# Three tiles of the third product in parts on even steps, and the left product rounded ahead of the relu of layer 0

## The reference

```python
e = stack([tbl_f[ids[:, f]] for f in range(32)], axis=1)        # (1024, 32, 64)
x0 = h = e
for i in (0, 1):
    z = einsum('bhd,bmd->bhmd', h, x0).reshape(batch, H * M, dim)
    out = relu(einsum('bcd,oc->bod', z, Ws[i]) + bs[i])          # 128 outputs
    # layer 0: the first 64 outputs are h of layer 1, the last 64 are a result
    # layer 1: all 128 are results
z = sum(concat(results, axis=1), axis=-1)                        # (1024, 192)
h = concat([z, dense_ctx], axis=1)
y = relu(relu(h @ W_top1 + b_top1) @ W_top2 + b_top2) @ W_top3
```

## Time and profile before

| | |
|---|---|
| median of 3 runs | 2003.78 us (2003.62 to 2006.34) |
| time of the profiled execution | 2002.59 us |
| its span on the core | 2000.7 us |
| mean granted TensorE clock | 0.997 of full speed |
| busy: TensorE, VectorE, ScalarE, GpSimd | 98%, 96%, 84%, 87% |
| mean traffic of DMA | 182 GB/s |

### The profile page before, as it was taken

How to read it: one execution, slowest core, us unless ns; L and a number is a source line. 1 busy time by engine, 2 the same in 40 slices (tenths; PEclk the granted TensorE clock), 3 DMA queues, 4 the chain that set the end, 5 groups by cost and what they waited for, 6 DMA issues and landing times.

```text
span 2000.7 us, 28399 instructions
## 1 busy us (share of the span) xinstructions
PE 1954.1 (98%) x7112; PEld 1338.9 (67%) x7112; DVE 1915.6 (96%) x1230; ACT 1687.7 (84%) x1943; POOL 1731.0 (87%) x708
## 2 busy tenths in 40 slices
PE   2999999999999999999999999999999999999998
PEld 0667666666666666666666666666676676676664
DVE  3999999999999999999999999999999999999991
ACT  2888888888888888888888888888888888888883
POOL 3998998998998998998998989989989989989871
PEclk9999999999999999999999999999999999999999
DMA  7998788788788788788887887887887887887820
GB/s 190 220 213 192 182 191 194 179 194 192 179 194 191 183 192 189 184 192 187 187 194 183 189 192 183 191 193 180 193 193 178 195 191 180 194 193 180 191 62 0
DMA packets 268305, 364.13 MB, mean 182 GB/s; under 512 B 107506, under 2 KB 107890, under 8 KB 268163
## 3 DMA queue, kind: packets, MB, share of 16 engines
q1 hardware_dynamic: 258338, 352.61, 77.5%
q0 software_dynamic: 8192, 8.40, 1.6%
q10 hardware_dynamic: 1760, 2.96, 0.5%
HBM read 347.02 MB, written 16.78 MB: 182 GB/s over the span
## 4 chain that ended last, share of the span: by engine, by line
PE 91%; POOL 4%; issue 2%; SPq 1%; DMA 1%; ACT 0%; DVE 0%; POOLq 0%
PE out L629 58%; PE out L613 20%; PE out L620 10%; POOL zl L217 4%; PE out L615 1%; SPq L259 0%; PE out L677 0%; DMA fields_dram<-emb 0%; POOL emb L200 0%; PE hrep L677 0%; SPq L284 0%; SPq L269 0%; PE out L670 0%; PE z L670 0%; PE hrep L670 0%
## 5 line engine op out<-in xcount | busy, mean ns | idle before, releaser
L217 POOL TENSOR_TENSOR zl<-prod,zh 128x2048 fp32r<-128x2048 f32 (+1 forms) x384 | 1473.2, 3866 | 144.2 <-ACT zh L372 144.1
L629 PE MATMUL out<-zh,w1h 128*128 128x512 f32 x1792 | 752.7, 420 | 5.5 <-DVE zl L512 4.4
L629 PE MATMUL out<-zl,w1h 128*128 128x512 f32 x1792 | 700.1, 391 | 0.0
L629 PE MATMUL out<-zh,w1l 128*128 128x512 f32 x1792 | 698.8, 390 | 0.0
L372 ACT ACTIVATE zh<-prod 128x2048 fp32r<-128x2048 f32 (+1 forms) x384 | 623.0, 1623 | 40.4 <-DVE prod L557 23.2
L385 ACT ACTIVATE hrep<-out,b_sb 32x512 f32<-32x512 f32 (+1 forms) x768 | 496.2, 646 | 131.9 <-PE out L615 122.1
L613 PE MATMUL out<-prod,w_sb 128*128 128x512 f32 x1024 | 464.6, 597 | 35.2 <-DVE prod L495 30.2
L629 PEld LDWEIGHTS out<-zh,w1h 128*128 128x128 f32 x1792 | 337.2, 188 | 130.4 <-issue 60.3
L629 PEld LDWEIGHTS out<-zh,w1l 128*128 128x128 f32 x1792 | 337.1, 188 | 97.8 <-issue 30.4
L629 PEld LDWEIGHTS out<-zl,w1h 128*128 128x128 f32 x1792 | 336.6, 188 | 73.8
L613 PEld LDWEIGHTS out<-prod,w_sb 128*128 128x128 f32 x1024 | 195.2, 191 | 232.3 <-issue 222.5
(11 more groups left out here) (61 smaller groups left out, 736.7 us busy)
## 6 DMA issues: line engine op xcount, KB each, us to landing
rot_low<-fields_dram SPq DMA_DIRECT2D x512, 256.0 KB, 6.7
rot_high<-fields_dram SPq DMA_DIRECT2D x512, 256.0 KB, 4.4
xrep<-fields_dram SPq DMA_DIRECT2D x256, 128.0 KB, 3.9
fields_dram<-emb SPq DMA_DIRECT2D x512, 32.0 KB, 5.3
left_x<-fields_dram SPq DMA_DIRECT2D x256, 64.0 KB, 2.9
left_y<-fields_dram SPq DMA_DIRECT2D x256, 64.0 KB, 2.2
emb<-in_tables,idx POOLq DMA_INDIRECT x256, 5.0
w_sb<-in_w ACTq DMA_DIRECT2D x1, 1024.0 KB, 6.2
```

The source lines that it names most:

```text
L217: pool.tensor_tensor(zl[u][:, :, :], product[:, 0:SIZES[u], :], zh[u][:, :, :].bitcast(F32), ALU.subtract).then_inc(zl_made[u], 1)
L629: mm = nc.tensor.matmul(out1[:, :], w[:, k, :], z[:, t, :], start=start and t == 0 and part == 0, stop=stop and t == SIZES[u] - 1 and part ...
```

## The change

Unit 2 gets three tiles of `prod[3]` in even steps and keeps two in odd ones; the whole tiles are then one in even steps and two in odd ones. ScalarE's rounding and GpSimd's subtraction of the unit are made as long as that. `round_left` moves on ScalarE from the start of the odd step, behind the copy of x, to the end of the even step before it, between `replicate_h1` and the relu of layer 0 (L402). The order on the other engines stays.

```diff
-SPLITS = (tiles(P1, 0, 4), tiles(P2, 0, 4), tiles(P3, 0, 2), tiles(P4, 0, 2), tiles(P4, 2, 4))
-SIZES = (4, 4, 2, 2, 2)
-FIRST = (0, 4, 8, 10, 12)
+SPLITS = (tiles(P1, 0, 4), tiles(P2, 0, 4), tiles(P3, 0, 3), tiles(P4, 0, 2), tiles(P4, 2, 4))
+SIZES = (4, 4, 3, 2, 2)
+FIRST = (0, 4, 8, 11, 13)
-WHOLE3 = tiles(P3, 2, 4)
+def in_parts(u, b):
+    return SIZES[u] - (u == 2 and b == 1)
...
-            def low_part(m, u, product):
+            def low_part(m, u, size, product):
...
-                pool.tensor_tensor(zl[u][:, :, :], product[:, 0:SIZES[u], :], zh[u][:, :, :].bitcast(F32),
+                pool.tensor_tensor(zl[u][:, 0:size, :], product[:, 0:size, :], zh[u][:, 0:size, :].bitcast(F32),
                                    ALU.subtract).then_inc(zl_made[u], 1)
...
-                act.activation(zh[u][:, :, :], product, ACT.Copy).then_inc(zh_made[u], 1)
+                act.activation(zh[u][:, 0:size, :], product[:, 0:size, :], ACT.Copy).then_inc(zh_made[u], 1)
...
-                if b == 1 and is_up_to(i, c, LAST - 1):
-                    round_left(i * 2 + (c + 1) // 2)
...
                 if is_up_to(i, c, LAST - 1):
                     replicate_h1(m + 1)
+                if b == 0 and is_up_to(i, c, LAST - 2):
+                    round_left(i * 2 + (c + 2) // 2)
+                if is_up_to(i, c, LAST - 1):
                     finish_l0(m + 1, 1 - b, i * 2 + (c + 1) // 2)
...
-            def whole(tiles, product, used):
-                for t in range(2):
-                    mm = nc.tensor.matmul(out1[:, :], w1_sb[:, tiles.start + t, :], product[:, t, :],
+            def whole3(m, b):
+                pe.wait_ge(p3_made, m + 1)
+                for t in range(in_parts(2, b), LOW):
+                    mm = nc.tensor.matmul(out1[:, :], w1_sb[:, tiles(P3, t, t + 1).start, :], prod[3][:, t, :],
                                           start=False, stop=False)
...
-            def split(m, u, start=False, stop=False):
+            def split(m, b, u, start=False, stop=False):
+                size = in_parts(u, b)
                 pe.wait_ge(zl_made[u], m + 1)
-                for t in range(SIZES[u]):
+                for t in range(size):
```

More of the change, by code:

```diff
@@ L227, in step @@
                     number_rows(n, b)
-                low_part(m, 0, prod[1])
-                low_part(m, 1, prod[2])
-                low_part(m, 2, prod[3])
+                low_part(m, 0, in_parts(0, c % HALVES), prod[1])
+                low_part(m, 1, in_parts(1, c % HALVES), prod[2])
+                low_part(m, 2, in_parts(2, c % HALVES), prod[3])
             pool.wait_ge(ids_loaded, 32)
@@ L366, in round_left, with round_split @@
                 act.activation(left_parts[:, :], lz[:, :], ACT.Copy).then_inc(left_rounded, 1)
-            def round_split(m, u, made, product):
+            def round_split(m, u, size, made, product):
                 act.wait_ge(made, m + 1)
@@ L411, in step @@
                     copy_left(i * 2 + (c + 2) // 2)
-                if b == 1 and is_up_to(i, c, LAST - 1):
-                    round_left(i * 2 + (c + 1) // 2)
-                round_split(m, 0, p1_made, prod[1][:, :, :])
-                round_split(m, 3, z4_made[0], z4[:, :, :])
+                round_split(m, 0, in_parts(0, b), p1_made, prod[1])
+                round_split(m, 3, in_parts(3, b), z4_made[0], z4)
                 if is_past(i, c, 0):
                     finish_l1(m - 1, 1 - b, i * 2 + (c + 1) // 2 - 1)
-                round_split(m, 1, p2_made, prod[2][:, :, :])
+                round_split(m, 1, in_parts(1, b), p2_made, prod[2])
                 if is_up_to(i, c, LAST - 1):
                     replicate_h0(m + 1)
-                round_split(m, 2, p3_made, prod[3][:, 0:SIZES[2], :])
-                round_split(m, 4, z4_made[1], z4[:, :, :])
+                round_split(m, 2, in_parts(2, b), p3_made, prod[3])
+                round_split(m, 4, in_parts(4, b), z4_made[1], z4)
                 if is_up_to(i, c, LAST - 1):
                     replicate_h1(m + 1)
+                if b == 0 and is_up_to(i, c, LAST - 2):
+                    round_left(i * 2 + (c + 2) // 2)
+                if is_up_to(i, c, LAST - 1):
                     finish_l0(m + 1, 1 - b, i * 2 + (c + 1) // 2)
@@ L616, in matmuls_l0 @@
                                  start=False, stop=True).then_inc(l0_done, 1)
-            def whole(tiles, product, used):
-                for t in range(2):
-                    mm = nc.tensor.matmul(out1[:, :], w1_sb[:, tiles.start + t, :], product[:, t, :],
+            def whole3(m, b):
+                pe.wait_ge(p3_made, m + 1)
+                for t in range(in_parts(2, b), LOW):
+                    mm = nc.tensor.matmul(out1[:, :], w1_sb[:, tiles(P3, t, t + 1).start, :], prod[3][:, t, :],
                                           start=False, stop=False)
-                mm.then_inc(used, 1)
-            def split(m, u, start=False, stop=False):
+                mm.then_inc(whole3_used, 1)
+            def split(m, b, u, start=False, stop=False):
+                size = in_parts(u, b)
                 pe.wait_ge(zl_made[u], m + 1)
-                for t in range(SIZES[u]):
+                for t in range(size):
                     k = FIRST[u] + t
@@ L629, in split @@
                         mm = nc.tensor.matmul(out1[:, :], w[:, k, :], z[:, t, :], start=start and t == 0 and part == 0,
-                                              stop=stop and t == SIZES[u] - 1 and part == 2)
+                                              stop=stop and t == size - 1 and part == 2)
                 mm.then_inc(split_used[u], 1)
@@ L635, in step @@
                 if is_past(i, c, 0):
-                    split(m - 1, 1)
-                    split(m - 1, 4)
-                    split(m - 1, 2, stop=True)
+                    split(m - 1, 1 - c % HALVES, 1)
+                    split(m - 1, 1 - c % HALVES, 4)
+                    split(m - 1, 1 - c % HALVES, 2, stop=True)
                 if is_up_to(i, c, LAST - 1):
@@ L642, in step @@
                     pe.wait_ge(relu1_made, m)
[L643 to L646, removed]
+                split(m, c % HALVES, 3, start=True)
+                split(m, c % HALVES, 0)
+                whole3(m, c % HALVES)
             pe.wait_ge(w0_folded, 4)
@@ L658, in _ @@
                 step(ITERS - 1, c)
-            split(LAST, 1)
-            split(LAST, 4)
-            split(LAST, 2, stop=True)
+            split(LAST, 1, 1)
+            split(LAST, 1, 4)
+            split(LAST, 1, 2, stop=True)
             pe.wait_ge(top_loaded, 96)
```

## The result

The changed kernel takes 1999.47 us in the median, the kernel before 2003.55 us, 20 runs each. The ratio is 0.9982 with a 95% interval of 0.9976 to 0.9988: 3.6 us less, between 2.4 and 4.8 (the medians themselves differ by 4.1). The profiled execution took 2000.27 us, with a span of 1998.4.

A forecast was written before the change was run, and what follows sets the result against it. TensorE was taken to bound the kernel at 29.92 us a pair, with VectorE's 29.875 taking over: 64 x (29.92 - 29.875) = 2.9 us less, so 2000.9 us predicted, range 1998.8 to 2003.9.

The forecast's parts named there:

- What bounds the kernel before: Over a pair of steps, TensorE sets the pace at 29.92 us; VectorE alone needs 29.875.
- TensorE's saving: In even steps, one whole tile becomes three float32r matmuls, saving 0.174 us; TensorE's pair falls to 29.75.
- VectorE's floor of 29.875: VectorE's own pair, read soon after the start where it catches up; it becomes the longest pair after the change.
- the gaps: Three late starts on VectorE around L505, 0.37 us a pair; moving the rounding gains 0.00. Rival that they close: chance 0.10.
- GpSimd: Subtracting three tiles takes 3.49 us, 1.11 more in even steps; its work becomes 29.07 a pair, under 29.875.
- ScalarE: Rounding three tiles takes 1.48 us, 0.45 more; `round_left` doesn't wait, and unit 0 of the odd step starts 0.22 later.
- the margins of 0.43 and 0.49 at unit 1: Time by which GpSimd's subtractions still precede TensorE's unit 1 loads: 0.43 us in even steps, 0.49 in odd.
- Queues: No DMA added; SyncE's loads start about 1.05 us later, covered by its average idle time of 2.2 for VectorE's L563.
- Start and end: Extra `w1` work at the start costs nothing; the last even step gives 0, between -0.5 and + 0.5 us.
- the sum: Over 64 pairs, 29.92 less 29.875 each gives 2.9 us less.
- the rule on held instructions: On VectorE, operands beginning in another 32-partition group than the last access wait for all earlier instructions; holds exactly three around L505.

The follow-up runs named there:

- The kernel before with L505 moved: The kernel before, with only L505 (the left product's subtraction) put on partitions 0 to 63 instead of 64 to 127: 2003.73 us, ratio 0.9999.
- the one with L505 moved as well: The kernel before plus the third tile in even steps and L505 on partitions 0 to 63, `round_left` in its old place: 1993.19 us, ratio 0.9945.
- 1992.37: The changed kernel with L505 on partitions 0 to 63 instead of 64 to 127: 1992.37 us, ratio 0.9943.
- 1999.32: The changed kernel without one of the two whole tiles of odd steps (not computed at all): 1999.32 us, ratio 0.9978.
- 1975.79: The changed kernel without one whole tile of odd steps and with L505 on partitions 0 to 63: 1975.79 us, ratio 0.9857.

## Why the prediction was right

*What bounds the kernel before: right.* TensorE, 29.92; freeing VectorE there changed nothing (0.9999), and moving one tile to the way that costs TensorE less gave the gain by itself.

*TensorE's saving: right.* 0.174 a pair was forecast; once VectorE was out of the way the pair measured 29.74, 0.18 less.

*VectorE's floor of 29.875: right, and the step on which all hung.* 29.873 measured, unmoved when TensorE had 0.86 less to do. In the trace of before it can be read only where TensorE doesn't hold VectorE back: after the start, and once more in the last pair, where the milestones are 29.87 apart (1939.02 - 1909.15). The kernel before with L505 moved has 29.49 in that last pair (1940.11 - 1910.62), again VectorE's pair without the gaps. The reading that the gaps belong to the instruction and are no wait was right too, 0.00 and not 0.37; the run with the move alone and those on the other partitions turn it from an argument into a finding.

*GpSimd: right.* 3.52 for three tiles where 3.49 was forecast, 0.34 of idle time left ahead of the odd batch where 0.2 to 0.4 was.

*ScalarE: the size right, the wait not seen.* Three tiles took 1.48. But `round_left` was said not to wait, and it waits 0.67 for the left product. The reckoning used the distances of before, in which VectorE is the one held back; after, TensorE and ScalarE run ahead of it until something of VectorE's stops them. For the same reason the margins of 0.43 and 0.49 at unit 1 are gone, and TensorE's loads wait there 0.60 - 0.24 = 0.36 and 0.40 - 0.24 = 0.16 instead. That costs nothing, since only engines that are ahead wait. It would have been the place to look if the time had gone up.

*Queues: right.* SyncE's idle time for VectorE's L563 is 230.1 / 122 = 1.9 on average, 0.3 less than before, and VectorE never waits for a load in the steady part.

*Start and end: the end was mis-sized.* I gave it 0, within half a microsecond. From the last milestone to the end of the span it was 2000.7 - 1939.02 = 61.68 before and 1998.4 - 1937.91 = 60.49 after, 1.2 less; it is 60.5 with the third tile alone too (1997.3 - 1936.80). In the last step VectorE's wait ahead of L517 is 0.73 and was 1.40: before the change VectorE was ahead of TensorE there, and what was left after its last milestone was TensorE's to do; after it TensorE is the one ahead. The pairs gave a little less than the sum had: from the milestone at 114.06 to the last it was 1939.02 - 114.06 = 1824.96 before, and 1937.91 - 115.64 = 1822.27 after, 2.7 less and not 2.9, since a few pairs before the change ran at 29.87 too. The two make 3.9, beside 3.6 (2.4 to 4.8) by the ratio and 4.1 by the medians. So the forecast lies inside the interval although it left out the 1.2 of the end.

The profiled execution shows only 2.3 less in its span: its milestone at 115.64 answers to one at 114.06 before, 1.6 us late. There TensorE's granted clock was 0.51 between 55 and 60 us, that is its lower level (1.2 GHz) for nearly all of the stretch, where it was 0.92 before:

```profile
55.00:60.00 5.00, 5.00 (x13) 3.89 (x12) 5.00 (x6) 4.32 (x7) 5.00 (x2) 0.51 1.13 253
```

The columns are the stretch, its length, the busy time of TensorE, its weight loads, VectorE, ScalarE and GpSimd with their counts, then the clock, the DMA share and the GB/s. In the 5 us before, TensorE had been busy for 2.57. The kernel with the third tile alone, and the one with L505 moved as well, had 0.94 and 0.84 in the stretch from 55 to 60 and reached the milestone at 114.65 and 114.45; the kernel before with L505 moved had 0.67 and reached it at 115.42, without any third tile. So the late milestone goes with the clock of that one execution more than with the change. Some tenths may be the change's own (114.65 and 114.45 against 114.06, and 114.21 with the move alone), which the prediction put at nothing; no run settles it.

The end of some runs holds a stretch at a lower granted clock too. In the profiled executions of the four kernels with 1992.37, 1999.32, 1975.79 and 1993.19 us the granted clock was 0.66 in 5 us about 25 us behind the last milestone, where TensorE had been idle for VectorE's last sum (2.12 us in the one with 1999.32). It was 1.00 in the kernel before and in the changed kernel, behind the same 2.12 us. In the one with 1999.32 the first two groups of perceptron matmuls there took 1.73 and 1.91 us, after the change 1.10 and 1.02, and the part behind the last milestone is 62.17 long where that of the changed kernel is 60.49. So up to 1.7 us of such a time may not be the edit's; the distances of milestones, on which the readings rest, don't hold it.

## What to carry to other kernels

Where two engines are within a per cent of each other, look for a stretch in which the second one runs free, after the start or after a disturbance; its distance there is the floor that a faster first engine will meet. A wait table points at engines that are ahead; follow each wait back until you reach the engine that has none. The page's chain can miss that engine: here it gave VectorE 0% in every run. A gap between starts that doesn't close when its releaser is early belongs to the instruction or its neighbours: ask what distinguishes their operands, before moving work around to feed it sooner.

## What was not expected of the hardware

That a change of the first partition alone (64 to 0) of one 64 x 512 subtraction is worth 0.38 us a pair on VectorE (2.31 + 0.73 + 1.26 against 2.19 + 0.60 + 1.13). There are three gaps of about 0.12: ahead of it, behind it, and ahead of the first instruction after it that writes SBUF. The prediction had it from the rule on held instructions (the Trainium skill, VectorE: DVE Perf Modes, "Two Vector instructions with no wait between them"), and the trace agrees in all three places, each start 0.03 to 0.04 behind the end of the instruction ahead. The prediction priced the gaps (1992.7 if they closed) but saw no way to close them; that one partition number does it, for some 7 us more than the change itself gives (1999.47 to 1992.37), was not foreseen.
